# Decay arguments from broadcast running sums in a Mamba-style mixer, instead of small matmuls

## The chip, the core and the metric

The kernel runs on one core of one Trainium2 chip. The metric is the device time of one execution in microseconds (us), median over runs. The core has a matrix engine (TensorE, PE in the profile, with its weight loads as PEld), a vector engine (VectorE, DVE), an activation engine (ScalarE, ACT), a general engine (GpSimd, POOL), a queue engine that here only issues transfers (SyncE, SP), and 16 DMA engines. The engines run side by side and wait for each other through semaphores; each executes its own list in order.

## The reference, cut to what matters

The whole computation is four residual blocks on x of shape (2, 512, 512): a block-sparse linear layer, a quantised feed-forward layer, a state-space mixer, and the feed-forward layer again. The change is in the mixer, which takes most of the time. Per batch, with H=128 heads of P=64 channels, G=8 groups of N=128 states and chunks of CS=128 tokens (four chunks):

```python
proj = hidden @ in_proj_w.T                  # gate z, x, B, C, dt
hBC = silu(conv4(hBC) + conv_b)              # depthwise over 4 tokens
dt = softplus(dt + dt_bias); A_dt = -exp(A_log) * dt
A_cumsum = cumsum(A_dt, axis=-1)             # inside each chunk, per head
Lmat = exp(segment_sum(A_dt))                # exp(cum[l] - cum[s]), 0 above the diagonal
Gm = einsum('clhn,cshn->clsh', C, B)
Y_diag = einsum('clsh,cshp->clhp', Gm * Lmat, x * dt)
states = einsum('clhn,clhp->chpn', B * exp(A_cumsum[-1] - A_cumsum), x * dt)  # carried over chunks
Y_off = einsum('clhn,chpn->clhp', C, states) * exp(A_cumsum)
y = Y_diag + Y_off + D * x;  y = rmsnorm(y) * norm_w * silu(gate);  out = y @ out_proj_w.T
```

The decay argument is the difference cum[l] - cum[s] for every pair of tokens in a chunk, 128 by 128 numbers per head and chunk. The kernel clamps it to at most zero before the exponential; what lies beyond the diagonal is then multiplied by zero in a mask.

## The kernel before, in words

The mixer runs as one block in which every engine has a hand-written list. It works in 128 steps k, one for each pair of heads in each of two batches (K = 128; 64 pairs for each batch). A step of TensorE is, in this order: project x for step k+1 (12 matmuls of 512 columns, L845), `outputs(k-1)` (L907, L913), `arguments(k)` (L870), `turn_x(k)` (L882), on one step in eight the Gram matrices of a new group, project z for k+1 (L845), `states(k)` (L893), on two neighbouring steps in eight a projection of B or C for the next group, and a share of the output projection (L926, 12 matmuls).

ScalarE's list in step k is `w_high` for the next x (L1022), `wo_high` (L1078), `tap` (L1034: first tap of the convolution out of the x projection), `w_high` for the next z, `exponent(k)` (L1060 clamps by Relu, L1062 takes Exp), `y_high` (L1072), `square` (L1066), `activate_x` (L1039), `activate_z` (L1044), and on two steps in eight a third `w_high`, then a `tap` of B or C. VectorE's list is `y_low` (L1249), `accumulate` (L1259), `decay_c` (L1222), `conv` (L1168, three instructions), `scale_x` (L1190, L1195), `gate` (L1239, L1243), `carry` (L1204, L1210), `mask_em` (L1230), and the convolution of B or C. GpSimd's list is `w_low` (L1347), `wo_low` (L1352), `w_low` for z, `sum_squares` (L1362), and on two steps in eight a third `w_low`.

Weights come in 256 KB tiles through two buffers (`w_raw`, NR = 2): SyncE issues the load of a tile only when GpSimd's `w_low` has finished with the tile two before it. PSUM banks for projections are used in a ring of three.

The decay arguments are made on TensorE. Before the steps begin, the running sums `cum` (heads on partitions) are split into three bf16 parts and stored to DRAM (`a_parts`). In each step SyncE loads six rows into `a_right` and six into `a_left` beside rows of ones, and eight bf16 matmuls of 128 columns write both heads' differences into the PSUM tile `ARG`. ScalarE clamps and exponentiates `ARG` in place, 1024 columns at a time. `ce`, a broadcast load of 384 KB of exp(cum), is already made per step by the same queue.

Of the kernel before, what the change touches and what calls it, by code (L numbers as in the profile page):

```python
# [8 lines left out]
BF16 = mybir.dt.bfloat16  # L9
# [38 lines left out]
def build(nc, x_in, mask_t, wa_t, bias_a, w_in, conv_w, conv_b, dt_bias, a_log, d_res, norm_w, w_out,  # L48
          gu_w, gu_z, gu_s, dn_w, dn_z, dn_s, x_mid, e_t, a_parts, out):
    with ExitStack() as ctx:  # L50
# [339 lines left out]
        mask_sb = sb("mask_sb", [P, KT, D], I32)  # L390
# [3 lines left out]
        block_on = sb("block_on", [P, KT * (D // BLK)])  # L394
        scope_a.close()
        early, sb = scope()
        wdt_raw = sb("wdt_raw", [P, KT * P])
# [11 lines left out]
        def load_early(sp):  # L409
            sp.dma_start(cw[:], conv_w).then_inc(m_w, 16)  # L410
            sp.dma_start(cb[:], conv_b).then_inc(m_w, 16)
            sp.dma_start(nw[:], norm_w).then_inc(m_w, 16)
            sp.dma_start(d_col[:], d_res).then_inc(m_w, 16)
            sp.dma_start(dtb_col[:], dt_bias.rearrange("o h -> h o")).then_inc(m_w, 16)
            sp.dma_start(wdt_raw[:], w_in[DT_T]).then_inc(m_w, 16)
            sp.dma_start(w_raw[:, 0], w_in[B_T]).then_inc(w_loaded[0], 16)
            sp.dma_start(w_raw[:, 1], w_in[C_T]).then_inc(w_loaded[1], 16)
# [197 lines left out]
        e_last = sb("e_last", [P, T, H])  # L615
# [14 lines left out]
        a_left = sb("a_left", [P, 2, 2, S], BF16)  # L630
        a_right = sb("a_right", [P, 2, 2, S], BF16)
# [10 lines left out]
        m_xn = sbp("m_xn", [P, 4, D])  # L642
        wdt = sbp("wdt", [P, 2, KT * P], F32R)
# [8 lines left out]
        rest = sbp("rest", [P, B * S])  # L652
        parts = sbp("parts", [P, 3, B * S], BF16)
# [14 lines left out]
        a_in, wdt_hi, wdt_lo = sem("a_log_loaded"), sem("wdt_hi"), sem("wdt_lo")  # L668
# [6 lines left out]
        parts_done, rest_done = sem("parts_done"), sem("rest_done")  # L675
# [5 lines left out]
        a_zero, a_ones = sem("a_zero"), sem("a_ones")  # L681
# [4 lines left out]
        arg_mm, arg_clamped, exp_done, em_done = sem("arg_mm"), sem("arg_clamped"), sem("exp_done"), sem("em_done")  # L686
# [85 lines left out]
        with nc.Block() as block:  # L772
            @block.sync
            def _(sp):
# [8 lines left out]
                def load_args(k):  # L783
                    b, h = batch(k), 2 * pair(k)
                    sp.wait_ge(a_ones, 4)
                    need(sp, arg_mm, k - 1)
                    sp.dma_start(a_right[0:3, k % 2], a_parts[0:3, h:h + 2, b * S:(b + 1) * S])\
                        .then_inc(a_loaded[k % 2], 16)
                    sp.dma_start(a_left[32:35, k % 2], a_parts[0:3, h:h + 2, b * S:(b + 1) * S])\
# [9 lines left out]

                sp.dma_start(a_neg[:], a_log.to_broadcast([P, H])).then_inc(a_in, 16)  # L800
                load_units(-1)
                load_units(0)
                for i in range(3):
                    if i == 2:
                        sp.wait_ge(cum_exp, 3)
                        sp.dma_start(e_t, e_cum[:]).then_inc(scratch_stored, 16)
                    sp.wait_ge(parts_done, i + 1)
                    sp.dma_start(a_parts[i], parts[:, i]).then_inc(scratch_stored, 16)
                sp.wait_ge(scratch_stored, 16 * 4)
# [13 lines left out]
            def _(pe):  # L823
# [40 lines left out]

                def arguments(k):
                    pe.wait_ge(a_loaded[k % 2], 32 * (k // 2 + 1))
                    need(pe, em_done, k)
# [5 lines left out]
                    mm.then_inc(arg_mm, 1)  # L873
# [88 lines left out]

                def spread_last():
# [29 lines left out]
                project(("x", 1))  # L993
                gram(0)
                spread_last()
                turn_dec()
                for k in range(STEPS):
                    if 0 < k < K - 1:
                        project(("x", k + 1))
                    if 1 <= k <= K:  # L1000
                        outputs(k - 1)
                    if k < K:
                        arguments(k)
# [12 lines left out]
            @block.scalar  # L1016
            def _(act):
# [82 lines left out]
                nc.scalar.activation(low[:], low[:], ACT.Ln, bias=1.0).then_inc(softplus, 1)  # L1100
                tap(("b", 0))
# [8 lines left out]
                nc.scalar.activation(parts[:, 0], cum[:].rearrange("p c l -> p (c l)"), ACT.Copy).then_inc(parts_done, 1)  # L1110
                nc.scalar.activation(e_end[:], cum[:, :, CS - 1], ACT.Exp).then_inc(cum_exp, 1)
                act.wait_ge(diff_done, 1)
# [3 lines left out]
                nc.scalar.activation(e_cum[:], cum[:].rearrange("p c l -> p (c l)"), ACT.Exp).then_inc(cum_exp, 1)  # L1116
                act.wait_ge(rest_done, 2)
                nc.scalar.activation(parts[:, 2], rest[:], ACT.Copy).then_inc(parts_done, 1)
# [6 lines left out]
                for b in range(B):  # L1125
                    act.wait_ge(last_mm, b + 1)
                    nc.scalar.activation(e_last[:, b * CPB:(b + 1) * CPB].rearrange("p c h -> p (c h)"), (ST, YT)[b][:],
# [29 lines left out]
            def _(dve):  # L1157
# [41 lines left out]
                def carry(k):  # L1199
# [5 lines left out]
                    for c in range(1, OFFC):  # L1205
                        dve.wait_ge(st_part, (2 * OFFC - 2) * k + 2 * c - 1)
                        for h in range(2):
# [5 lines left out]
                                scalar=e_last[:, batch(k) * CPB + c, at:at + 1],  # L1213
# [97 lines left out]
                dve.wait_ge(parts_done, 1)  # L1311
                nc.vector.tensor_tensor(rest[:], cum[:].rearrange("p c l -> p (c l)"), parts[:, 0], ALU.subtract)                    .then_inc(rest_done, 1)
                dve.wait_ge(parts_done, 2)
                dve.wait_ge(rest_done, 1)
                nc.vector.tensor_tensor(rest[:], rest[:], parts[:, 1], ALU.subtract).then_inc(rest_done, 1)
# [27 lines left out]
            def _(pool):  # L1343
# [10 lines left out]

                def sum_squares(k):
# [8 lines left out]
                nc.gpsimd.memset(a_left[:].bitcast(F32), 0.0).then_inc(a_zero, 1)  # L1364
                nc.gpsimd.memset(a_right[:].bitcast(F32), 0.0).then_inc(a_zero, 1)
                pool.wait_ge(a_zero, 2)
                for j in range(2):
                    nc.gpsimd.memset(a_left[0:3, j], 1.0).then_inc(a_ones, 1)
                    pool.wait_ge(a_ones, 2 * j + 1)
                    nc.gpsimd.memset(a_right[32:35, j], -1.0).then_inc(a_ones, 1)  # L1370
                    pool.wait_ge(a_ones, 2 * j + 2)
                pool.wait_ge(wdt_hi, 1)
                nc.gpsimd.tensor_tensor(wdt[:, 1], wdt_raw[:], wdt[:, 0].bitcast(F32), ALU.subtract).then_inc(wdt_lo, 1)
                w_low(("b", 0))
# [9 lines left out]
                pool.wait_ge(cum_exp, 2)  # L1384
# [3 lines left out]
                for k in range(STEPS):  # L1388
# [140 lines left out]
```

## Time and profile before

| | |
|---|---|
| Median of 3 runs | 2247.12 us (2246.6 to 2247.6) |
| The profiled execution | 2251.26 us, span 2249.5 us |
| PE / PEld / DVE busy | 95% / 78% / 73% |
| ACT / POOL busy | 62% / 40% |
| DMA: moved, share of 16 engines (hardware queue) | 239.72 MB, 33.2% |

The span runs from the first to the last instruction of the profiled execution; the time of that execution has 1.8 us more around it. The mixer's steps run from about 357 us to 1960 us of the span. In the rows, times at the left are starts in us from the span's start, and the second number is how long the merged instructions took; brackets show how long the engine had been idle before and what released it.

### The profile page before, as it was taken

The page shows a single profiled execution, that of the slowest core. Times are in us where ns is not written, and L with a number is a line of the kernel's source. Part 1 is how long each engine was busy: PE and PEld are TensorE (multiplying, and loading weights), DVE is VectorE, ACT ScalarE, POOL GpSimd, SP SyncE. Part 2 cuts the span into 40 slices and gives each one's busy share as a digit, 9 for nine tenths or more (in the row PEclk, how much of TensorE's full clock was granted, in tenths as well). Part 3 has the DMA queues.
Part 4 walks back from the last instruction along what each step waited for, and adds up shares of the span by engine and source line. Part 5 has one row for each costly group of instructions (what it writes and reads, how often), then busy time and mean ns, then how long its engine had stood idle before and what let it go on. Part 6 is the DMA issues. An engine that isn't in the chain of part 4 may idle for free. (4 is left out here: it accounts for less than half of the span.)

```text
span 2249.5 us, 37149 instructions
## 1 busy us (share of the span) xinstructions
PE 2137.5 (95%) x13374; PEld 1765.6 (78%) x13374; DVE 1639.2 (73%) x2683; ACT 1390.0 (62%) x1872; POOL 907.6 (40%) x639
## 2 busy tenths in 40 slices
PE   5999986899999999999999999999999999959999
PEld 4788865788888888888888888888888888748887
DVE  8655466778787777778787777778787877755554
ACT  2222236777777777777777777777777777622221
POOL 2222123454444545454444445454454445342221
PEclk9999988999999999999999999999999999979999
DMA  4434313333333233233333333333332333323431
GB/s 164 138 132 150 103 59 104 101 106 92 111 93 110 97 103 102 94 104 102 101 106 97 107 96 107 96 103 100 95 107 96 107 95 108 120 89 136 168 131 75
DMA packets 127794, 241.87 MB, mean 108 GB/s; under 512 B 13200, under 2 KB 47760, under 8 KB 127376
## 3 DMA queue, kind: packets, MB, share of 16 engines
q1 hardware_dynamic: 127632, 239.72, 33.2%
q8 instruction: 100, 1.64, 0.3%
q14 instruction: 62, 0.51, 0.1%
HBM read 234.17 MB, written 5.51 MB: 107 GB/s over the span
## 5 line engine op out<-in xcount | busy, mean ns | idle before, releaser
L845 PE MATMUL ring<-m_lnt,w_sb 128*128 128x512 f32 x3456 | 853.3, 396 | 15.9 <-DVE xc L1168 15.9
L845 PEld LDWEIGHTS ring<-m_lnt,w_sb 128*128 128x128 f32 x3456 | 639.1, 189 | 149.3 <-DVE xc L1168 19.6
L1347 POOL TENSOR_TENSOR w_sb<-w_raw,w_sb 128x512 fp32r<-128x512 f32 x288 | 434.6, 1514 | 337.0 <-ACT w_sb L1022 336.5
L1168 DVE SCALAR_TENSOR_TENSOR xc<-ring,cw,xc 128x511 f32<-128x511 f32 (+2 forms) x384 | 287.3, 748 | 185.7 <-ACT xc L1034 176.7
L926 PE MATMUL ring<-wo,ygs 128*128 128x512 f32 x1536 | 383.1, 399 | 2.5 <-POOL wo L1352 2.5
L1362 POOL TENSOR_TENSOR ysq<-ysq,y 128x512 f32<-128x512 f32 x126 | 163.8, 1300 | 531.3 <-ACT y L1066 531.3
L926 PEld LDWEIGHTS ring<-wo,ygs 128*128 128x128 f32 x1536 | 282.5, 189 | 60.7 <-issue 3.1
L1022 ACT ACTIVATE w_sb<-w_raw 128x512 fp32r<-128x512 f32 x288 | 177.1, 621 | 33.6 <-DMA w_raw<-w_in 33.6
L1034 ACT ACTIVATE xc<-ring,cb,cw 128x512 f32<-128x512 f32 x128 | 99.2, 775 | 146.8 <-PE ring L845 146.8
L1060 ACT ACTIVATE arg<-arg 128x1024 f32<-128x1024 f32 x128 | 129.0, 1008 | 90.4 <-PE arg L870 90.4
L907 PE MATMUL yt<-em,x_dt 128*64 128x128 f32 x2048 | 183.6, 279 | 1.2 <-DVE em L1230 1.2
L365 PE MATMUL bank_e<-f_lnt,f_gu 128*128 128x512 f32 x672 | 159.8, 399 | 11.2 <-DVE f_lnt L135 6.5
L1352 POOL TENSOR_TENSOR wo<-wo_raw,wo 128x512 fp32r<-128x512 f32 x128 | 168.6, 1317 | 3.3 <-ACT wo L1078 3.3
L288 POOL TENSOR_TENSOR f_gu<-f_gu_f,f_gu 128x1024 fp32r<-128x1024 f32 x28 | 67.3, 2404 | 251.8 <-ACT f_gu L312 251.8
L1062 ACT ACT_TABLE_LOAD x128 | 164.2, 1283 | 2.4
L1039 ACT ACT_TABLE_LOAD x127 | 162.9, 1283 | 2.3
L365 PEld LDWEIGHTS bank_e<-f_lnt,f_gu 128*128 128x128 f32 x672 | 130.1, 194 | 39.7 <-issue 10.5
L365 PE MATMUL bank<-f_lnt,f_gu 128*128 128x512 f32 x672 | 154.1, 390 | 3.4 <-DVE f_hf L251 1.8
L1230 DVE TENSOR_TENSOR em<-arg,gt 128x1024 f32<-128x1024 f32 x128 | 155.9, 1218 | 0.1
L907 PEld LDWEIGHTS yt<-em,x_dt 128*64 128x64 f32 x2048 | 118.0, 136 | 46.4 <-issue 43.3
L365 PEld LDWEIGHTS bank<-f_lnt,f_gu 128*128 128x128 f32 x672 | 125.9, 188 | 30.3 <-issue 4.0
L913 PE MATMUL yt<-ce,state 128*64 128x128 f32 x1536 | 149.1, 273 | 0.0
(178 smaller groups left out, 3131.3 us busy)
## 6 DMA issues: line engine op xcount, KB each, us to landing
w_raw<-w_in SPq DMA_DIRECT2D x288, 256.0 KB, 4.4
ce<-e_t SPq DMA_DIRECT2D x128, 384.0 KB, 4.3
wo_raw<-w_out SPq DMA_DIRECT2D x128, 256.0 KB, 4.5
f_gu_q<-gu_w SPq DMA_DIRECT2D x28, 512.0 KB, 5.3
f_gu_zr<-gu_z SPq DMA_DIRECT2D x28, 512.0 KB, 6.6
f_gu_sr<-gu_s SPq DMA_DIRECT2D x28, 512.0 KB, 8.0
f_dn_q<-dn_w SPq DMA_DIRECT2D x28, 256.0 KB, 7.1
f_dn_zr<-dn_z SPq DMA_DIRECT2D x28, 256.0 KB, 7.5
```

The source lines that it names most:

```text
L365: mm = nc.tensor.matmul(dst[half][:], gu[:, j, b, c:c + P], lnt[:, a, k, half * TOK:(half + 1) * TOK], start=(i == 0), stop=(i == 3 * KT - 1))
L845: mm = nc.tensor.matmul(dst[:], w_sb[:, u % WR, wp, k * P:(k + 1) * P], lnt[:, xp, k, b * S:(b + 1) * S], start=(i == 0), stop=(i == 3 * K ...
L907: mm = nc.tensor.matmul(YT[h * HD:(h + 1) * HD, c * CS:(c + 1) * CS], x_dt[:, at:at + HD], em[:, h, c * CS:(c + 1) * CS], start=True, stop ...
L926: mm = nc.tensor.matmul(dst[:], ygs[:, j % OR, yp, t * P:(t + 1) * P], wo[:, j % WOR, wp], start=(m == 0), stop=(m == 3 * HALF - 1))
L1022: nc.scalar.activation(w_sb[:, u % WR, 0], w_raw[:, u % NR], ACT.Copy).then_inc(w_hi, 1)
L1039: nc.scalar.activation(xc[:, k % 3], xc[:, k % 3], ACT.Silu).then_inc(silu_x, 1)
L1062: nc.scalar.activation(part, part, ACT.Exp, scale=-1.0).then_inc(exp_done, 1)
L1168: nc.vector.scalar_tensor_tensor(out=dst[:, d:S], in0=src[:, 0:S - d], scalar=cw[:, tile, j:j + 1], in1=dst[:, d:S], op0=ALU.mult, op1=ALU ...
L1230: nc.vector.tensor_tensor(em[:], ARG[:], gt[:, k // QG % 2].rearrange("p (o t) -> p o t", o=1).to_broadcast([P, 2, S]), ALU.mult).then_inc ...
L1347: nc.gpsimd.tensor_tensor(w_sb[:, u % WR, 1], w_raw[:, u % NR], w_sb[:, u % WR, 0].bitcast(F32), ALU.subtract).then_inc(w_lo, 1)
L1352: nc.gpsimd.tensor_tensor(wo[:, j % WOR, 1], wo_raw[:, j % 2], wo[:, j % WOR, 0].bitcast(F32), ALU.subtract).then_inc(wo_lo, 1)
L1362: nc.gpsimd.tensor_tensor(part, part, y[:, k % 2], ALU.add).then_inc(ysq_done, 1)
```

## The change

The matmuls of the decay argument, their operands, the bf16 split and the memsets that prepared the operands are taken out. In their place:

- The running sums are stored to DRAM once as they are (`a_t`), and each step loads both heads' rows, 512 tokens each, broadcast over all 128 partitions into `a_row` (512 KB). The load waits for `exp_done` of two steps back.
- Before the steps, TensorE transposes `cum` once (8 transposes) and VectorE copies the result into `a_q`, a column for each step, chunk and head.
- `exponent(k)`: ScalarE takes Relu of a_q - a_row for the first head, four instructions of 128 columns with a per-partition bias, then Exp of it (512 columns, into PSUM), waits for GpSimd, and takes Exp of the second head.
- `clamp_second(k)`: GpSimd subtracts a_q from a_row and takes the minimum with 0 for the second head, four instructions of 128 columns. It stands behind `w_low` of the z tile.
- `e_cum` is exponentiated earlier in the preparation; `wdt_raw` is loaded at the start of the mixer instead of long before it, so the first weights are split in another order; `e_last` keeps two of four chunks for each batch.

```diff
 load_args(k):
-    sp.wait_ge(a_ones, 4)
-    need(sp, arg_mm, k - 1)
-    sp.dma_start(a_right[0:3, k % 2], a_parts[0:3, h:h + 2, b * S:(b + 1) * S])...
-    sp.dma_start(a_left[32:35, k % 2], a_parts[0:3, h:h + 2, b * S:(b + 1) * S])...
+    need(sp, exp_done, k - 1)
+    sp.dma_start(a_row[:, k % 2], a_t[h:h + 2, b * S:(b + 1) * S]
+                 .rearrange("(o h) t -> o h t", o=1).to_broadcast([P, 2, S]))...
...
 TensorE, before the steps:
+    for b in range(B):
+        for c in range(CPB):
+            mm = nc.tensor.transpose(ARG[:, b, c * H:(c + 1) * H], cum[:, b * CPB + c], ident[:])
 TensorE, each step:
-    for h in range(2):
-        for c in range(CPB):
-            mm = nc.tensor.matmul(ARG[:, h, c * CS:(c + 1) * CS],
-                                  a_left[:, k % 2, h, c * CS:(c + 1) * CS],
-                                  a_right[:, k % 2, h, c * CS:(c + 1) * CS], start=True, stop=True)
...
 exponent(k):
-    act.wait_ge(arg_mm, k + 1)
-    part = ARG[:].rearrange("p h t -> p (h t)")
-    nc.scalar.activation(part, part, ACT.Relu, scale=-1.0).then_inc(arg_clamped, 1)
-    act.wait_ge(arg_clamped, k + 1)
-    nc.scalar.activation(part, part, ACT.Exp, scale=-1.0).then_inc(exp_done, 1)
+    act.wait_ge(a_loaded[k % 2], 16 * (k // 2 + 1))
+    need(act, em_done, k)
+    for c in range(CPB):
+        nc.scalar.activation(a_row[:, k % 2, 0, c * CS:(c + 1) * CS],
+                             a_row[:, k % 2, 0, c * CS:(c + 1) * CS], ACT.Relu,
+                             bias=a_q[:, k, c, 0:1], scale=-1.0).then_inc(arg_first, 1)
+    act.wait_ge(arg_first, CPB * (k + 1))
+    nc.scalar.activation(ARG[:, 0], a_row[:, k % 2, 0], ACT.Exp, scale=-1.0)
+    act.wait_ge(arg_second, CPB * (k + 1))
+    nc.scalar.activation(ARG[:, 1], a_row[:, k % 2, 1], ACT.Exp).then_inc(exp_done, 1)
...
+clamp_second(k), on GpSimd behind w_low of the z tile and ahead of sum_squares(k - 1):
+    pool.wait_ge(a_loaded[k % 2], 16 * (k // 2 + 1))
+    for c in range(CPB):
+        nc.gpsimd.tensor_scalar(a_row[:, k % 2, 1, c * CS:(c + 1) * CS],
+                                a_row[:, k % 2, 1, c * CS:(c + 1) * CS],
+                                a_q[:, k, c, 1:2], 0.0, ALU.subtract, ALU.min).then_inc(arg_second, 1)
...
 ScalarE, before the steps (a copy of each of the three parts, Exp of e_cum in between):
-    nc.scalar.activation(parts[:, 0], cum..., ACT.Copy).then_inc(parts_done, 1)
     nc.scalar.activation(e_end[:], cum[:, :, CS - 1], ACT.Exp).then_inc(cum_exp, 1)
+    nc.scalar.activation(e_cum[:], cum..., ACT.Exp).then_inc(cum_exp, 1)
     act.wait_ge(diff_done, 1)
     nc.scalar.activation(diff[:], diff[:], ACT.Exp).then_inc(cum_exp, 1)
-    act.wait_ge(rest_done, 1)
-    nc.scalar.activation(parts[:, 1], rest[:], ACT.Copy).then_inc(parts_done, 1)
-    nc.scalar.activation(e_cum[:], cum..., ACT.Exp).then_inc(cum_exp, 1)
-    act.wait_ge(rest_done, 2)
-    nc.scalar.activation(parts[:, 2], rest[:], ACT.Copy).then_inc(parts_done, 1)
```

## Rows read from the trace of the kernel before

**Rows 1.** Windows, one stretch of the steps: busy time and count of each engine, clock, DMA.

```profile
600.00:900.00 300.00, 296.97 (x2061) 246.90 (x2060) 237.11 (x401) 228.75 (x304) 143.50 (x102) 1.00 0.33 100
```

**Rows 2.** Waits, 600 to 1500 us: total us, times, longest.

```profile
ACT arg L1060 <- PE arg L870: 50.5, 54, 0.9
...
ACT w_sb L1022 <- DMA w_raw<-w_in: 16.8, 8, 2.2
```

**Rows 3.** Timeline of an ordinary step (PEld left out).

```profile
860.22 0.78 ACT L1034 ACTIVATE xc<-ring,cb,cw 128x512 f32<-128x512 f32 x1 [1.31 <-PE ring L845]
...
861.59 1.27 POOL L1347 TENSOR_TENSOR w_sb<-w_raw,w_sb 128x512 fp32r<-128x512 f32 x1
861.79 0.62 PE L870 MATMUL arg<-a_right,a_left 128*128 128x128 bf16 x8
...
862.25 0.61 PE L882 MATMUL xt<-ident,xc 128*128 128x128 f32 x4
...
862.45 1.01 ACT L1060 ACTIVATE arg<-arg 128x1024 f32<-128x1024 f32 x1 [0.94 <-PE arg L870]
...
863.26 0.55 DVE L1190 TENSOR_TENSOR x_dec<-xt,dec_q 128x384 f32<-128x384 f32 x1
...
864.77 1.01 ACT L1062 ACTIVATE arg<-arg 128x1024 f32<-128x1024 f32 x1
865.10 0.75 DVE L1243 SCALAR_TENSOR_TENSOR sz<-y,nw,sz 128x512 f32<-128x512 f32 x1
865.46 0.83 PE L893 MATMUL st<-x_dec,b_tok 128*128 128x128 f32 x6
865.88 0.63 ACT L1072 ACTIVATE ygs<-sz 128x512 fp32r<-128x512 f32 x1
...
869.88 0.95 DVE L1222 TENSOR_TENSOR ce<-ce,bc 128x768 f32<-128x768 f32 x1
...
873.39 0.62 PE L870 MATMUL arg<-a_right,a_left 128*128 128x128 bf16 x8
```

**Rows 4.** Timeline of the two steps with B and C projections (PEld left out).

```profile
897.95 0.63 ACT L1022 ACTIVATE w_sb<-w_raw 128x512 fp32r<-128x512 f32 x1 [2.16 <-DMA w_raw<-w_in]
...
898.66 1.30 POOL L1347 TENSOR_TENSOR w_sb<-w_raw,w_sb 128x512 fp32r<-128x512 f32 x1 [1.02 <-ACT w_sb L1022]
...
900.81 1.01 ACT L1062 ACTIVATE arg<-arg 128x1024 f32<-128x1024 f32 x1
...
906.53 2.32 DVE L1168 SCALAR_TENSOR_TENSOR bc<-ring,cw,bc 128x511 f32<-128x511 f32 x3 [2.96 <-ACT bc L1034]
...
910.76 2.03 DVE L1222 TENSOR_TENSOR ce<-ce,bc 128x768 f32<-128x768 f32 x1
...
915.54 0.94 PE L893 MATMUL st<-x_dec,b_tok 128*128 128x128 f32 x6 [0.81 <-DVE x_dec L1190]
```

**Rows 5.** Groups of instructions by shape, GpSimd: count, busy us, mean ns.

```profile
L115 POOL TENSOR_SCALAR f_n_xn<-xr,f_n_mv,f_n_rstd 128x512 f32<-128x512 f32 x8 | 16.9, 2124 | 30.5 <-DVE f_n_rstd L109 24.8 <-PE bank_e L123 5.7
...
L1360 POOL COPY ysq<-y 128x512 f32<-128x512 f32 x2 | 1.2, 612 | 8.5 <-ACT y L1066 8.5
```

**Rows 6.** Groups of instructions by shape, ScalarE.

```profile
L1034 ACT ACTIVATE xc<-ring,cb,cw 128x512 f32<-128x512 f32 x128 | 99.2, 775 | 146.8 <-PE ring L845 146.8
...
L1044 ACT ACT_TABLE_LOAD x1 | 1.3, 1283 | 0.0
...
L1095 ACT ACTIVATE a_neg<-a_neg 128x128 f32<-128x128 f32 x1 | 0.3, 313 | 0.0
```

**Rows 7.** Timeline of the preparation before the first step.

```profile
334.79 0.60 ACT L1108 ACTIVATE cum<-arg 128x512 f32<-128x512 f32 x1 [0.30 <-PE arg L959]
...
348.44 1.05 ACT L1049 ACTIVATE bc<-bc 128x1024 f32<-128x1024 f32 x1
...
349.54 2.08 PE L855 MATMUL ring<-bc 128*128 128x128 f32 x8 [12.05 <-ACT bc L1049]
```

**Rows 8.** The page's DMA queue: packets, MB, share of 16 engines.

```profile
q1 hardware_dynamic: 127632, 239.72, 33.2%
```

More of the change, by code:

```diff
@@ L8 @@
 F32R = mybir.dt.float32r
-BF16 = mybir.dt.bfloat16
 I32 = mybir.dt.int32
@@ L394, in build @@
         block_on = sb("block_on", [P, KT * (D // BLK)])
+        mask_sb = sb("mask_sb", [P, KT, D], I32)
         scope_a.close()
         early, sb = scope()
-        wdt_raw = sb("wdt_raw", [P, KT * P])
         cw = sb("cw", [P, CONV // P, TAPS])
@@ L614, in build @@
         dec_q = sb("dec_q", [P, K, CPB, 2])
-        e_last = sb("e_last", [P, T, H])
+        a_q = sb("a_q", [P, K, CPB, 2])
+        e_last = sb("e_last", [P, B * (OFFC - 1), H])
         banks_ctx.close()
@@ L629, in build @@
         b_tok = sb("b_tok", [P, 2, OFFC * NS])
-        a_left = sb("a_left", [P, 2, 2, S], BF16)
-        a_right = sb("a_right", [P, 2, 2, S], BF16)
+        a_row = sb("a_row", [P, 2, 2, S])
         ce = sb("ce", [P, 2, 2, OFFC * CS])
@@ L642, in build @@
         m_xn = sbp("m_xn", [P, 4, D])
+        wdt_raw = sbp("wdt_raw", [P, KT * P])
         wdt = sbp("wdt", [P, 2, KT * P], F32R)
@@ L651, in build @@
         e_cum = sbp("e_cum", [P, B * S])
-        rest = sbp("rest", [P, B * S])
-        parts = sbp("parts", [P, 3, B * S], BF16)
         e_end = sbp("e_end", [P, T])
@@ L685, in build @@
         gram_mm, btok_mm, gt_done, btok_done = sem("gram_mm"), sem("btok_mm"), sem("gt_done"), sem("btok_done")
-        arg_mm, arg_clamped, exp_done, em_done = sem("arg_mm"), sem("arg_clamped"), sem("exp_done"), sem("em_done")
+        arg_first, arg_second = sem("arg_first"), sem("arg_second")
+        exp_done, em_done = sem("exp_done"), sem("em_done")
         xt_mm, xdt_done, xdec_done = sem("xt_mm"), sem("xdt_done"), sem("xdec_done")
@@ L802, in _ @@
                 load_units(0)
[L803 to L809, printed above, removed]
+                sp.wait_ge(cum_done, B)
+                sp.dma_start(a_t, cum[:].rearrange("p c l -> p (c l)")).then_inc(scratch_stored, 16)
+                sp.wait_ge(cum_exp, 2)
+                sp.dma_start(e_t, e_cum[:]).then_inc(scratch_stored, 16)
+                sp.wait_ge(scratch_stored, 16 * 2)
                 load_args(0)
@@ L961, in cumulate, with turn_cum @@
                         mm.then_inc(cum_mm, 1)
+                def turn_cum():
+                    pe.wait_ge(cum_done, B)
+                    for b in range(B):
+                        for c in range(CPB):
+                            mm = nc.tensor.transpose(ARG[:, b, c * H:(c + 1) * H], cum[:, b * CPB + c], ident[:])
+                        mm.then_inc(cumt_mm, 1)
                 def spread_last():
@@ L993, in _ @@
                 project(("x", 1))
+                turn_cum()
                 gram(0)
@@ L1002, in _ @@
                     if k < K:
-                        arguments(k)
                         turn_x(k)
@@ L1089, in _ @@
                 w_high(("b", 0))
+                act.wait_ge(wdt_loaded, 16)
+                nc.scalar.activation(wdt[:, 0], wdt_raw[:], ACT.Copy).then_inc(wdt_hi, 1)
                 for t in range(T):
@@ L1100, in _ @@
                 nc.scalar.activation(low[:], low[:], ACT.Ln, bias=1.0).then_inc(softplus, 1)
+                act.wait_ge(m_w, 16 * 5)
                 tap(("b", 0))
@@ L1109, in _ @@
                 act.wait_ge(cum_done, B)
-                nc.scalar.activation(parts[:, 0], cum[:].rearrange("p c l -> p (c l)"), ACT.Copy).then_inc(parts_done, 1)
                 nc.scalar.activation(e_end[:], cum[:, :, CS - 1], ACT.Exp).then_inc(cum_exp, 1)
+                nc.scalar.activation(e_cum[:], cum[:].rearrange("p c l -> p (c l)"), ACT.Exp).then_inc(cum_exp, 1)
                 act.wait_ge(diff_done, 1)
                 nc.scalar.activation(diff[:], diff[:], ACT.Exp).then_inc(cum_exp, 1)
-                act.wait_ge(rest_done, 1)
-                nc.scalar.activation(parts[:, 1], rest[:], ACT.Copy).then_inc(parts_done, 1)
-                nc.scalar.activation(e_cum[:], cum[:].rearrange("p c l -> p (c l)"), ACT.Exp).then_inc(cum_exp, 1)
-                act.wait_ge(rest_done, 2)
-                nc.scalar.activation(parts[:, 2], rest[:], ACT.Copy).then_inc(parts_done, 1)
                 tap(("x", 1))
@@ L1126, in _ @@
                     act.wait_ge(last_mm, b + 1)
-                    nc.scalar.activation(e_last[:, b * CPB:(b + 1) * CPB].rearrange("p c h -> p (c h)"), (ST, YT)[b][:],
+                    nc.scalar.activation(e_last[:, b * (OFFC - 1):(b + 1) * (OFFC - 1)].rearrange("p c h -> p (c h)"),
+                                         (ST, YT)[b][:, H:OFFC * H],
                                          ACT.Copy).then_inc(last_done, 1)
@@ L1212, in carry @@
                                 in0=state[:, c - 1, h * HD:(h + 1) * HD],
-                                scalar=e_last[:, batch(k) * CPB + c, at:at + 1],
+                                scalar=e_last[:, batch(k) * (OFFC - 1) + c - 1, at:at + 1],
                                 in1=ST[:, c * PAIR + h * HD:c * PAIR + (h + 1) * HD],
@@ L1310, in _ @@
                 conv(("x", 0))
[L1311 to L1315, printed above, removed]
+                for b in range(B):
+                    dve.wait_ge(cumt_mm, b + 1)
+                    nc.vector.tensor_copy(a_q[:, b * JP:(b + 1) * JP],
+                                          ARG[:, b].rearrange("p (c j h) -> p j c h", c=CPB, h=2)).then_inc(aq_done, 1)
                 mask_gram(0)
@@ L1353, in wo_low, with clamp_second @@
                                             ALU.subtract).then_inc(wo_lo, 1)
+                def clamp_second(k):
+                    pool.wait_ge(a_loaded[k % 2], 16 * (k // 2 + 1))
+                    if k == 0:
+                        pool.wait_ge(aq_done, B)
+                    for c in range(CPB):
+                        nc.gpsimd.tensor_scalar(a_row[:, k % 2, 1, c * CS:(c + 1) * CS],
+                                                a_row[:, k % 2, 1, c * CS:(c + 1) * CS],
+                                                a_q[:, k, c, 1:2], 0.0, ALU.subtract, ALU.min).then_inc(arg_second, 1)
                 def sum_squares(k):
@@ L1362, in sum_squares @@
                         nc.gpsimd.tensor_tensor(part, part, y[:, k % 2], ALU.add).then_inc(ysq_done, 1)
[L1364 to L1371, printed above, removed]
+                w_low(("b", 0))
                 pool.wait_ge(wdt_hi, 1)
                 nc.gpsimd.tensor_tensor(wdt[:, 1], wdt_raw[:], wdt[:, 0].bitcast(F32), ALU.subtract).then_inc(wdt_lo, 1)
-                w_low(("b", 0))
                 w_low(("c", 0))
@@ L1395, in _ @@
                         w_low(unit)
+                    if k < K:
+                        clamp_second(k)
                     if 1 <= k <= K:
```

28 lines of the change are left out of this document (10 added, 18 removed).

## The prediction, as it was put on record

> **What bounds the kernel now.** I read the table of stretches first. In 300 us of the steps TensorE is busy 296.97 us at a granted clock of 1.00, while VectorE has 237, ScalarE 229 and GpSimd 143.5 [rows 1]. So the mixer is bound by TensorE's list, and a shorter list is worth something as long as the other lists keep up. The waits then show how near they are. In 900 us ScalarE waits 50.5 us for the argument matmuls and 16.8 us, in 8 waits of up to 2.2 us, for a weight tile [rows 2]. Those 8 waits recur once in eight steps, so I looked at two timelines: an ordinary step, and the two neighbouring steps that also project B or C.
>
> In the ordinary step two starts of L870 lie 873.39 - 861.79 = 11.60 us apart, and TensorE stands still nowhere for another engine. Its nearest dependence is `x_dec`: VectorE has it at 863.81, TensorE asks at 865.46, a slack of 1.65 us. ScalarE has two holes, 1.31 us before `tap` and 0.94 us before L1060 [rows 3]. In the other two steps it is different. ScalarE takes the z tile only at 897.95, after 2.16 us of waiting for its DMA; everything in its list behind that is late, the convolution of B starts after 2.96 us of idleness, and at 915.54 TensorE waits 0.81 us for `x_dec` [rows 4]. I call these the chain steps; with the Gram step behind them they are three of eight. The last group has none, so there are 15 such groups, and about 80 ordinary steps of the 128 are left after the irregular first ones.
>
> **What goes from TensorE.** From the first argument matmul to the first transpose is 862.25 - 861.79 = 0.46 us [rows 3]; the 0.62 us of the group's busy time overlaps the next one. The wait on semaphores ahead of the arguments now stands ahead of `turn_x`, and I charge about 0.05 us for it, an estimate. That leaves 0.41 us a step. In 80 ordinary steps this is 33 us; in all steps but the first it would be 52 us.
>
> **What ScalarE gets.** Out go two instructions of 1.01 us; in come four Relus of 128 columns and two Exps of 512. The nearest rows for a Relu are 0.313 us (128 columns, no scalar from memory) and 0.775 us (512 columns, two scalars from memory) [rows 6]; I take 0.38 us each, and 0.28 from start to start since successive rows of this engine overlap by about 0.1. That makes about 1.15 us, and 0.5 to 0.6 for an Exp. With the table load of 1.28 between them [rows 6] this is about 0.3 us more than before. The 0.94 us hole ahead of it is gone, because `a_row` has long been loaded, so alone it costs nothing in an ordinary step; cover gone, it would be 0.3 us in each of 45 chain steps at most, 14 us.
>
> **What GpSimd gets, and what waits for it.** This is the disputed price. The trace has no clamp of 128 columns. The one tensor-with-scalar instruction on GpSimd takes 2.1 us for 512 columns; the copy takes 0.61 [rows 5]. Scaled by columns with 0.1 us fixed, one clamp is 0.6 us by the first and 0.23 by the second. If nothing of the first shrinks with the columns it is 2.1. I take c = 0.6 us, since it is the same operation with another second step, and keep 0.15 to 2.1 as bounds.
>
> Four clamps start when `w_low` of z ends, and the second Exp, 0.62 us, waits for all four, with 0.05 us for the hand-over (both estimates). Ordinary step: 861.59 + 1.27 + 0.05 + 4c + 0.62 = 863.53 + 4c, so 865.93 for c = 0.6. `y_high` started at 865.88 anyway, because it waits for `sz`, which VectorE ends at 865.85 [rows 3]. So nothing moves. ScalarE's own round becomes 11.60 - 1.31 - (865.88 - 863.53) + 4c = 7.94 + 4c, or 10.3 us for c = 0.6, against a TensorE round of 11.60 - 0.41 = 11.19. It fits until c = 0.81.
>
> Chain step: the z tile comes late from DMA, and that time is set by GpSimd and the queue, not by TensorE. `w_low` ends at 899.96, so the second Exp ends at 900.63 + 4c = 903.03, where it ended at 901.82 before [rows 4]. That is 4c - 1.19 = 1.2 us later, and behind the Exp stand `y_high`, `square`, both Silus, the next two weight tiles and the tap of B; then the convolutions and `x_dec`. TensorE already waits at this place, so the delay arrives, and TensorE's own saving in the three steps is spent in waiting. 15 x 1.2 = 18 us lost.
>
> The Trainium skill speaks for a smaller c: its page "GPSIMD Engine Reference", section "Engine selection", says that one-input elementwise work on GpSimd runs roughly at line rate, and section "Elementwise" gives 769 ns for 512 elements as its best case. An estimate from that figure is 0.2 to 0.25 us per clamp, and the sum would end at -34 us in place of -21. The row of 2.1 us for 512 columns speaks against it.
>
> **Port and queues.** `decay_c`, with both inputs in SBUF, takes 0.95 us in the ordinary step [rows 3] and 2.03 us in a chain step that is otherwise the same [rows 4], where a `w_low` of GpSimd runs at the time; the three instructions of `conv`, with one input in PSUM, take 2.32 us in total. The clamps lie from 862.9 to 865.3, over `conv`, `scale_x` and the first `gate` instruction, which read PSUM; only `sz` at 865.10 may be held, for about 0.2 us, within the slack. I charge nothing. On SyncE `a_row` stands where the two small loads stood and waits for an older event than `ce` behind it does. It adds 128 x 0.524 = 67 MB to 239.72 MB that take 33.2% of the DMA engines [rows 8]: in proportion that is 9.3 points more, about 43%. No queue fills; the price is only a burst. The critical z tile is issued before the next `a_row`, so I charge nothing; if a tile did wait behind one, it would be 0.524 MB at 321 GB/s (239.72 MB in 0.332 x 2249.5 us) = 1.6 us, 24 us over 15 groups.
>
> **The preparation.** From 334.79 to 348.44 ScalarE makes the sums, three bf16 parts with two waits for VectorE, and the activations for the first Gram matrix, and TensorE stands 12.05 us [rows 7]. Without the parts ScalarE's list is cum, a table load 1.28, `e_end` at about 0.2 and `e_cum` and `diff` at 1.01 each like L1060, a tap of 0.78, a weight tile of 0.63, a table load 1.28, a Silu of z at 0.6 [rows 3, 4, 6]: from 335.39 on that is 6.8 us, and the Silu of B and C starts at about 342 instead of 348.44. That is 6 us; the first clamp group gives perhaps 1 back, the removed memsets and the moved weight load change the start by under 1 in either direction. The 8 transposes and two copies of `a_q` fall into the hole. I take -6.
>
> **Sum.** -33 + 18 - 6 = -21 us against the profiled execution's 2251.3 us, which is 4.1 us above the median; against the median of 2247.1 us that is 2226 us. With c from 0.52 to 0.67 and 6 us for the rest of the terms the likeliest case spans 2214 to 2240.
>
> **Rivals.**
> 1. *Short clamps.* At c = 0.25 the chain steps lose only ScalarE's own 0.3 us: -33 + 5 - 6 = -34, so 2213 us. For it: the copy row, and the page named above. Against it: the row of 2.1 us. Chance 0.17.
> 2. *The whole saving arrives.* If the chain steps are in truth set by TensorE, 52 us and the 6 come in full: 2189 us. For it: its wait there is only 0.81 us [rows 4]. Against it: the DMA wait ahead of them does not depend on TensorE. Chance 0.10.
> 3. *Slower: GpSimd becomes the bound.* If a large part of the 2.1 us is fixed, c exceeds 0.81, ScalarE's round 7.94 + 4c passes TensorE's, and the sum crosses zero near c = 0.83. At c = 1.0: 80 x 0.34 + 15 x 2.81 - 6 = +63, so 2310 us; at 2.1 it is over 2700. For it: it is four instructions where the row has one, each with its own start and its own scalar. Against it: the copy shows no large fixed part. Chance 0.17.
> 4. *The burst.* Loads of 512 KB hold weight tiles back: -21 + 24 = +3, so 2250 us, no change. For it: 16.8 us of waits for these tiles already [rows 2]. Against it: the order of issue. Chance 0.08.
>
> My forecast has 0.45, and 0.03 is left for the rest. A difference under 0.2%, 4.5 us, cannot be told from none. Faster: 0.45 + 0.17 + 0.10 = 0.72; within 0.2%: 0.08; slower: 0.20. The range goes from 2190, the edge of rival 2, to 2265, which takes in rival 4 and rival 3 up to c of about 0.87.
>
> **What would show it.** L870 is gone and ordinary steps are 11.2 us apart (if 11.6 or more: rival 3). A clamp takes 0.6 us; the second Exp ends at most 0.1 us before `y_high`. In the chain steps the wait of TensorE for `x_dec` or a bank grows to some 2 to 3 us per group, and ScalarE's wait for GpSimd appears before the second Exp. The wait of 12.05 us before the first Gram matrix halves. ScalarE's waits for `w_raw` stay near 17 us per 900 (if they double: rival 4). The prediction fails most easily by c, at 60 us of time for each us of c, and far more beyond 0.81.

## The result: 2303 us, slower

| | before | after |
|---|---|---|
| Median of 4 runs | 2246.99 us | 2302.97 us (2297.41 to 2311.72) |
| Ratio, 95% interval | | 1.0242, 1.0224 to 1.026 |
| The profiled execution | 2251.26 us, span 2249.5 | 2311.72 us, span 2310.0 |

The profiled execution is the longest of the four. The predicted time was 2226 us, the range ended at 2265. The page of the changed kernel, busy time of the engines and the DMA queue (beside the table ahead of the prediction and [rows 8]):

```profile
PE 2112.5 (91%) x12358; PEld 1717.4 (74%) x12358; DVE 1738.3 (75%) x2683; ACT 1419.5 (61%) x2381; POOL 1257.3 (54%) x1145
...
q1 hardware_dynamic: 159856, 305.00, 40.5%
```

One stretch of its windows, which answers to [rows 1]:

```profile
600.00:900.00 300.00, 276.91 (x1787) 225.24 (x1786) 246.26 (x384) 225.95 (x382) 198.36 (x188) 1.00 0.42 135
```

TensorE has 25 us less work in all and is no longer busy throughout: 277 of 300 us, at the same granted clock. GpSimd has 350 us more. Its waits from 600 to 1500 us, beside [rows 2]:

```profile
ACT arg L1059 <- POOL a_row L1353: 151.4, 69, 2.6
...
PE st L876 <- DVE x_dec L1184: 28.2, 29, 2.2
...
ACT w_sb L1012 <- DMA w_raw<-w_in: 24.6, 14, 2.7
...
PE ring L838 <- ACT sz L1034: 23.9, 9, 2.8
```

The wait for the argument matmuls, 50.5 us, is gone, and one of 151.4 us for GpSimd stands in its place: every Exp of the second head waits (69 times in 900 us, which are 68 to 69 steps of 13.1 us on average). Behind it TensorE waits for `x_dec` and for a bank that a late Silu of z holds. The new instructions, by shape:

```profile
L1353 POOL TENSOR_SCALAR a_row<-a_row,a_q 128x128 f32<-128x128 f32 x512 | 404.6, 806 | 0.0
...
L1053 ACT ACTIVATE a_row<-a_row,a_q 128x128 f32<-128x128 f32 x512 | 162.5, 392 | 0.0
```

A clamp takes 0.81 us, not 0.6; a Relu 0.39, as reckoned. The timeline of an ordinary step shows what the clamps close (TensorE, VectorE and weight loads left out):

```profile
871.12 0.60 ACT L1059 ACTIVATE arg<-a_row 128x512 f32<-128x512 f32 x1 [2.56 <-POOL a_row L1353]
...
875.12 0.62 ACT L1012 ACTIVATE w_sb<-w_raw 128x512 fp32r<-128x512 f32 x1
...
875.82 1.50 POOL L1340 TENSOR_TENSOR w_sb<-w_raw,w_sb 128x512 fp32r<-128x512 f32 x1 [1.66 <-ACT w_sb L1012]
...
877.28 1.30 POOL L1345 TENSOR_TENSOR wo<-wo_raw,wo 128x512 fp32r<-128x512 f32 x1
...
878.54 1.29 POOL L1340 TENSOR_TENSOR w_sb<-w_raw,w_sb 128x512 fp32r<-128x512 f32 x1
...
879.81 3.25 POOL L1353 TENSOR_SCALAR a_row<-a_row,a_q 128x128 f32<-128x128 f32 x4
...
883.09 0.60 ACT L1059 ACTIVATE arg<-a_row 128x512 f32<-128x512 f32 x1 [2.56 <-POOL a_row L1353]
```

From one step's Exp of the second head to the next step's is a closed round (a chain of work that leads from an instruction back to the same one a step later) with no gap in it: ScalarE from the Exp to the high part of the next x tile, 4.70 us up to GpSimd's start; three subtractions, 3.99; four clamps, 3.25; hand-over 0.03. That is 11.97 us, where TensorE alone would need 11.17. The step with the late tile, beside [rows 4]:

```profile
915.21 0.63 ACT L1012 ACTIVATE w_sb<-w_raw 128x512 fp32r<-128x512 f32 x1 [2.46 <-DMA w_raw<-w_in]
...
917.18 3.22 POOL L1353 TENSOR_SCALAR a_row<-a_row,a_q 128x128 f32<-128x128 f32 x4
...
920.43 0.60 ACT L1059 ACTIVATE arg<-a_row 128x512 f32<-128x512 f32 x1 [1.51 <-POOL a_row L1353]
...
924.59 2.79 PE L838 MATMUL ring<-m_lnt,w_sb 128*128 128x512 f32 x11 [2.56 <-ACT sz L1034]
```

TensorE stands 2.56 us there for the Silu of z, which follows the late Exp in ScalarE's list. The preparation, beside [rows 7]:

```profile
345.11 2.08 PE L848 MATMUL ring<-bc 128*128 128x128 f32 x8 [4.53 <-ACT bc L1039]
```

The hole of 12.05 us is now 4.53. In this execution the first transpose of step 0 starts 4.6 us earlier than before, from there to the first transpose of the last step it takes 63.2 us more, and what follows takes 1.9 us more: 60.5 us, the difference of the two spans. Where the 63.2 lie is seen from the starts of the first transpose of each step, which I took from the traces. The table has the mean distance to the next step by place in the group of eight, over 14 groups (the first and the last left out); places 3 to 5 are the chain steps.

| us | 0 | 1 | 2 | 3 | 4 | 5 | 6 | 7 | group |
|---|---|---|---|---|---|---|---|---|---|
| before | 11.60 | 11.60 | 11.60 | 14.32 | 14.77 | 13.82 | 11.60 | 11.60 | 100.91 |
| after | 11.15 | 11.91 | 11.92 | 18.64 | 15.39 | 13.78 | 11.17 | 11.17 | 105.13 |
| e1 | 11.17 | 11.17 | 11.17 | 13.94 | 16.46 | 13.45 | 11.17 | 11.17 | 99.68 |
| e2 | 11.17 | 11.17 | 11.17 | 14.31 | 16.54 | 13.24 | 11.17 | 11.17 | 99.93 |
| e3 | 13.56 | 13.40 | 13.29 | 16.02 | 16.50 | 18.22 | 11.17 | 12.32 | 114.49 |
| e4 | 11.16 | 11.89 | 11.91 | 18.50 | 15.49 | 13.81 | 11.17 | 11.17 | 105.10 |
| e5 | 11.17 | 11.17 | 11.17 | 13.89 | 15.51 | 13.88 | 11.17 | 11.17 | 99.11 |
| e6 | 11.17 | 11.17 | 11.17 | 14.25 | 16.86 | 13.24 | 11.17 | 11.17 | 100.18 |
| e7 | 11.17 | 11.17 | 11.17 | 13.89 | 16.09 | 13.67 | 11.17 | 11.17 | 99.48 |
| e8 | 11.17 | 11.17 | 11.17 | 14.39 | 16.18 | 13.55 | 11.17 | 11.17 | 99.96 |
| e9 | 11.17 | 11.91 | 11.87 | 16.51 | 16.95 | 13.13 | 11.17 | 11.17 | 103.87 |
| e10 | 11.18 | 11.86 | 11.17 | 15.28 | 17.31 | 12.83 | 11.17 | 11.17 | 101.97 |
| e11 | 11.17 | 11.17 | 11.17 | 13.89 | 14.07 | 13.88 | 11.17 | 11.17 | 97.67 |
| e12 | 11.60 | 11.60 | 11.60 | 14.32 | 14.32 | 12.82 | 11.60 | 11.60 | 99.46 |

Three ordinary places (6, 7 and 0) got TensorE's 0.43 us. Places 1 and 2 lost 0.3 each to the round, and place 3 lost 4.3. The round is as long in those three places as in the others: from one Exp of the second head to the next it is 11.9 to 12.0 us in places 5, 6, 7, 0 and 1 (means over the same groups). Behind the chain steps TensorE comes late and the round has slack; at 11.17 us a step for TensorE it loses 0.8 us of that slack in each of places 6, 7 and 0, and from place 1 on TensorE waits for it.

The clock is not the cause. In its steps (all but the first 20 us of them) the changed kernel spent 24 us at the lower level, a granted clock of 0.50, that is 1.2 GHz, and the kernel before 3 us; but e1 below has the same 24 us and is some 80 us faster.

### The profile page after: what moved, and what is told of

Read it like the earlier page. It is cut to its first block and busy times, and to the rows that moved or that the text cites. A ratio compares the mean times of both kernels' runs of the same rounds, so it can differ in the third digit from the quotient of the medians.

```text
span 2310.0 us, 35876 instructions
## 1 busy us (share of the span) xinstructions
PE 2112.5 (91%) x12358; PEld 1717.4 (74%) x12358; DVE 1738.3 (75%) x2683; ACT 1419.5 (61%) x2381; POOL 1257.3 (54%) x1145
## 5 line engine op out<-in xcount | busy, mean ns | idle before, releaser
L1340 POOL TENSOR_TENSOR w_sb<-w_raw,w_sb 128x512 fp32r<-128x512 f32 x288 | 393.9, 1372 | 362.8 <-ACT w_sb L1012 362.8
L1353 POOL TENSOR_SCALAR a_row<-a_row,a_q 128x128 f32<-128x128 f32 x512 | 404.6, 806 | 0.0
L1059 ACT ACTIVATE arg<-a_row 128x512 f32<-128x512 f32 x128 | 77.1, 602 | 278.8 <-POOL a_row L1353 278.8
L1243 DVE TENSOR_TENSOR ygs<-sz,ygs 128x512 fp32r<-128x512 f32 x128 | 199.3, 1557 | 0.7 <-ACT ygs L1069 0.7
L876 PEld LDWEIGHTS st<-x_dec,b_tok 128*128 128x128 f32 x768 | 100.7, 193 | 89.2 <-DVE x_dec L1184 84.9
L876 PE MATMUL st<-x_dec,b_tok 128*128 128x128 f32 x768 | 113.9, 285 | 57.6 <-DVE x_dec L1184 57.5
L1053 ACT ACTIVATE a_row<-a_row,a_q 128x128 f32<-128x128 f32 x512 | 162.5, 392 | 0.0
```

The source lines that it names most:

```text
L876: mm = nc.tensor.matmul(ST[:, c * PAIR:(c + 1) * PAIR], b_tok[:, k // QG % 2, c * NS:(c + 1) * NS], x_dec[:, c * PAIR:(c + 1) * PAIR], sta ...
L1243: nc.vector.tensor_tensor(ygs[:, k % OR, 1], sz[:, k % 3], ygs[:, k % OR, 0].bitcast(F32), ALU.subtract).then_inc(yg_lo, 1)
L1340: nc.gpsimd.tensor_tensor(w_sb[:, u % WR, 1], w_raw[:, u % NR], w_sb[:, u % WR, 0].bitcast(F32), ALU.subtract).then_inc(w_lo, 1)
L1353: nc.gpsimd.tensor_scalar(a_row[:, k % 2, 1, c * CS:(c + 1) * CS], a_row[:, k % 2, 1, c * CS:(c + 1) * CS], a_q[:, k, c, 1:2], 0.0, ALU.su ...
```

## The experiments

Medians of four runs each, beside the median of the kernel before on the same chip at the time (2245.4 for e1 to e4, 2247.1 for e5 to e8, 2244.8 for e9 to e12). The changed kernel's 2303.0 was measured beside 2247.0, so up to some 2 us of a difference between groups of runs can be the chip's.

### e1 to e4: clamps, their wait, their engine, the loads

e1, no clamps of the second head:

```diff
-                    act.wait_ge(arg_second, CPB * (k + 1))
...
-                    if k < K:
-                        clamp_second(k)
```

> The changed kernel without the four GpSimd clamps and without the wait for them: the second head's exponential is taken of the loaded sums as they are, so its decay argument is left out of the computation. Theory G (the clamps close a round through GpSimd: weight high part on ScalarE, three subtractions and four clamps on GpSimd, Exp, the next weight high part, 8.7 us and four clamps of 0.81, and they also make the step after the late weight tile longer): ordinary steps 11.17 us apart in all places, the step with the late tile near 14.4, the whole 2205 to 2220 us. Theory D (the 512 KB load of each step holds weight tiles back): the time stays above 2280 us, with ScalarE's waits for weight tiles near 25 us per 900.

Measured 2221.5 us, ratio 0.9896 (0.988 to 0.9913). All ordinary places are at 11.17, place 3 is at 13.94 (14.4 was expected): theory G holds, D falls. The total is 1.5 us above what I gave; place 4 is longer than I thought.

e2, the same clamps one step ahead:

```diff
+                clamp_second(0)
                 for k in range(STEPS):
...
-                    if k < K:
-                        clamp_second(k)
+                    if k + 1 < K:
+                        clamp_second(k + 1)
```

> All of the computation, the same four clamps on GpSimd at the same place of its list, but for the second head of the next step, so that no exponential waits for the clamps just issued. Theory G: the wait is the cost and not GpSimd's time as such, so nearly all comes back: 2205 to 2225 us, ScalarE's wait for GpSimd ahead of the second Exp gone. Rival P (GpSimd's added 3.2 us of work delays weights or holds VectorE's instructions with two inputs in SBUF): 2250 us or more. Theory D: above 2280 us.

Measured 2230.0 us, 0.9932 (0.9916 to 0.9949), 5 us above what theory G gave: some 70 us of the changed kernel's time gone with GpSimd's work unchanged. It was the wait, not the work. Rival P has a small part: 8.5 us above e1.

e3, the clamps on VectorE:

```diff
                         decay_c(k)
+                        clamp_second(k)        # nc.vector, waits and operands as on GpSimd
                     if k + 1 < K:
                         conv(("x", k + 1))
```

> All of the computation, the four clamps of the second head on VectorE between decay_c and the convolution of x, where VectorE had a hole of 1.79 us in an ordinary step. Theory G: a clamp of 128 columns is short there (0.2 to 0.3 us, a guess from the 0.54 us of VectorE's 512-column instruction of this kind), so 2205 to 2225 us. If VectorE's list is as near to TensorE's as GpSimd's was: x_dec late, 2235 us or more. Theory D: above 2280 us.

Measured 2450.4 us, 1.0911 (1.0892 to 1.0929), a miss of over 200 us by theory G. The other branch, `x_dec` late, came true (TensorE waits 72.1 us for it from 600 to 1500 us), but with no upper bound it foretold little. The tile's durations (minimum, median, maximum in ns) and a stretch of the timeline show why:

```profile
L1225 DVE TENSOR_SCALAR a_row<-a_row,a_q x512: 271/1298/1371, 347.0 to 2146.7; 128x128 f32<-128x128 f32 x171
```

```profile
910.91 1.50 POOL L1350 TENSOR_TENSOR w_sb<-w_raw,w_sb 128x512 fp32r<-128x512 f32 x1 [1.65 <-ACT w_sb L1012]
911.20 3.99 DVE L1225 TENSOR_SCALAR a_row<-a_row,a_q 128x128 f32<-128x128 f32 x4
...
912.37 1.28 POOL L1355 TENSOR_TENSOR wo<-wo_raw,wo 128x512 fp32r<-128x512 f32 x1
...
913.61 1.30 POOL L1350 TENSOR_TENSOR w_sb<-w_raw,w_sb 128x512 fp32r<-128x512 f32 x1
```

The 211 clamps that overlap no GpSimd instruction take 0.274 us on average; the 301 that do have a median of 1.31 us (mean 1.26), the length of one GpSimd subtraction. While GpSimd subtracts three tiles in a row, four clamps need 3.99 us: three of them let one whole instruction pass each, and the fourth takes 0.27. The lower clock has a small part in e3: its steps have 140 us at the lower level, those of e7 14. Over e3's 14 groups each us at that level goes with 0.12 us more, so an estimate of its share is 15 us.

e4, the rows loaded for two steps only:

```diff
-                    need(sp, exp_done, k - 1)
-                    sp.dma_start(a_row[:, k % 2], ...)
+                    if k < 2:
+                        sp.dma_start(a_row[:, k % 2], ...)
```

> The changed kernel with the rows of sums loaded only for the first two steps; all later steps work on what lies in the buffers, so their decay arguments are left out of the computation; every clamp and wait between the engines stays. Theory G: 2295 to 2305 us, as changed. Theory D: the 67 MB are the cost, so 2240 us or less, and ScalarE's waits for weight tiles fall to 17 us per 900 or less.

Measured 2302.8 us, 1.0254 (1.0237 to 1.0271): the changed kernel's time. Theory D is out; the 67 MB cost nothing that can be measured in this kernel.

### e5 to e8: the ceiling, a dose, two other ways

e5, the kernel before without the matmuls:

```diff
                     if k < K:
-                        arguments(k)
                         turn_x(k)
...
-                    act.wait_ge(arg_mm, k + 1)
+                    act.wait_ge(a_loaded[k % 2], 32 * (k // 2 + 1))
+                    need(act, em_done, k)
```

> The kernel before with the eight argument matmuls of each step left out (the decay argument is then not computed; ScalarE clamps and exponentiates what lies in ARG, with waits for the loads and for mask_em instead); GpSimd, the DMAs and ScalarE's two instructions of 1024 columns stay. It prices TensorE's part alone. Theory G with the chain steps set elsewhere: ordinary steps 11.17 us apart and the three others as long in sum as before, so 34 us saved, 2205 to 2215 us. Rival F (the whole saving arrives, 0.43 us in 127 steps): 2190 to 2196 us.

Measured 2220.5 us, 0.9883 (0.9867 to 0.99): 26.7 us saved, so the time is 5.5 us above my band. Ordinary steps give 0.43 us each, and the three chain steps are 0.37 us longer in sum than before (43.28 against 42.91). So what the matmuls are worth there is all waited away, as the prediction had it, and rival F, its rival 2, is out.

e6, one clamp of 512 columns:

```diff
-                    for c in range(CPB):
-                        nc.gpsimd.tensor_scalar(a_row[:, k % 2, 1, c * CS:(c + 1) * CS], ..., a_q[:, k, c, 1:2], ...)
+                    nc.gpsimd.tensor_scalar(a_row[:, k % 2, 1], a_row[:, k % 2, 1], a_q[:, k, 0, 1:2], ...)
```

> The changed kernel with one clamp of 512 columns for each step in place of four of 128 (all four chunks take the column of the first, so the decay arguments of three chunks are not the right ones). A dose: GpSimd spends 2.1 us in place of 3.2. Theory G: the round through GpSimd falls from 11.92 to about 10.8 us, under TensorE's 11.17, so ordinary steps come at 11.17 throughout (1.5 us a group), and the step with the late tile loses 1.1 us: 15 x 2.6 = 39 us less, about 2264 us. Rival P (the port shared with VectorE decides): one long instruction holds VectorE longer than four short ones, 2290 us or more.

Measured 2230.8 us, 0.9921 (0.9905 to 0.9938):

```profile
L1352 POOL TENSOR_SCALAR a_row<-a_row,a_q x128: 1978/1997/2707, 351.1 to 1931.8; 128x512 f32<-128x512 f32 x128
```

The ordinary steps did what theory G said. But I gave 1.1 us to place 3 and it fell by 4.4; the total is 33 us under my 2264, and the response to 1.2 us of GpSimd's time is 72 us. Once the round is under TensorE's, no lag is left to carry into place 3. From 128 and 512 columns the price of a clamp follows: 0.705 us (the trace's shortest are 0.702) and 1.997, so 3.4 ns a column and 0.27 us fixed; the 0.81 on average in the changed kernel includes 118 clamps of 0.79 to 1.4 us, 108 of which overlap the second `gate` instruction of VectorE; the 30 that overlap none take 0.71.

e7, VectorE again, at another place:

```diff
                         mask_em(k)
+                    if k + 1 < K:
+                        clamp_second(k + 1)    # nc.vector
```

> All of the computation, the clamps of the second head on VectorE as in e3, but for the next step and behind mask_em, where GpSimd has nothing to do. Theory P for e3 (a VectorE clamp takes 0.27 us, and 1.3 us only where it must let a whole GpSimd subtraction pass): nearly all clamps take 0.27 us, ordinary steps 11.17 us, 2215 to 2230 us. Rival V (VectorE's own list is too long by the clamps): x_dec late, ordinary steps over 11.5 us, 2260 us or more.

Measured 2219.8 us, 0.9874 (0.9857 to 0.989), the time of e5. The same instructions as in e3, 230 us apart by their place in VectorE's list (some 15 of them the clock's):

```profile
L1225 DVE TENSOR_SCALAR a_row<-a_row,a_q x512: 269/278/1367, 347.7 to 1917.7; 128x128 f32<-128x128 f32 x171
```

e8, one subtraction for both heads:

```diff
+                    nc.gpsimd.tensor_tensor(part, part, a_q[:, k].rearrange("p c (h o) -> p h c o", o=1)
+                                            .to_broadcast([P, 2, CPB, CS]), ALU.subtract).then_inc(arg_second, 1)
...
+                    nc.scalar.activation(row, row, ACT.Relu, scale=-1.0).then_inc(arg_first, 1)
+                    act.wait_ge(arg_first, k + 1)
+                    nc.scalar.activation(part, row, ACT.Exp, scale=-1.0).then_inc(exp_done, 1)
```

> All of the computation in another form: one GpSimd subtraction of 1024 columns for both heads with a_q broadcast over columns, one step ahead, then one Relu and one Exp of 1024 columns on ScalarE. GpSimd about 2.4 us a step in place of 3.0, ScalarE about 0.3 us less than in the changed kernel. If ScalarE's longer list is what the chain steps lose in e1 and e2: 2208 to 2220 us. If the port decides (a two-input subtraction holds VectorE longer): 2230 us or more.

Measured 2230.0 us, 0.9922 (0.9906 to 0.9939), the time of e2 and at the edge of its rival's band. The subtraction is shorter than thought (median 1.905 us), ScalarE's list is too, and nothing came of it. So ScalarE's extra 0.3 us is not what the chain steps lose in e2; what e2 and e8 share and e7 lacks is GpSimd's work and, in 900 us, 39.6 us (e8) and 44.7 us (e2) in which GpSimd waits for the row load. The runs don't part the two.

### e9 to e12: what makes place 3 so long, and what sets the chain steps

e9 and e10 leave the clamps out at place 3, or at places 1 and 2:

```diff
+        def clamped(k):
+            return k % QG not in (3,)          # e10: (1, 2)
...
-                    if k < K:
+                    if k < K and clamped(k):
                         clamp_second(k)
```

> The changed kernel without the clamps, and the wait for them, in one step of eight: the one with the late weight tile (its second head's argument is then not made). Theory G1 (that step's growth by 4.3 us is mostly its own clamps standing behind the late tile): the step falls from 18.6 to about 14.5 to 15.5 us and the next by a little, 2245 to 2255 us. Theory G2 (the growth is lag carried in from the two steps ahead): the step stays above 17 us, 2280 us or more.

> The changed kernel without the clamps in the two steps ahead of the late tile (their second head's argument is then not made). Both fall from 11.92 to 11.17 us, 1.5 us a group. Theory G1: the step with the late tile stays at 17.5 us or more, 2275 to 2282 us. Theory G2: it falls to 15.5 or less, 2250 us or less.

Measured: e9 2286.8 us, 1.0196 (1.0177 to 1.0215); e10 2259.2 us, 1.007 (1.0053 to 1.0087). Of the two places that were to fall to 11.17 in e10 only place 2 did; place 1 stays at 11.86, because its lag comes from the clamps of the steps ahead of it, which are still there. Places 3 to 5 sum to 47.81 us in the changed kernel, 46.59 in e9, 45.42 in e10 and 43.85 in e1. Of the 3.96 us that clamps cost there, those of place 3 bring 1.2, and those of the two steps ahead bring 2.4 as lag carried in. Neither theory was right in full: G2 gave the larger part, but place 3 fell to 16.5 in e9, and e10's total is 9 us above G2's bound.

e11 is e7, and e12 the kernel before, with the third weight tile's high part ahead of the Silus:

```diff
                         square(k - 1)
+                    for unit in ahead[2:]:
+                        w_high(unit)
                     if k + 1 < K:
                         activate_x(k + 1)
                         activate_z(k + 1)
-                    for unit in ahead[2:]:
-                        w_high(unit)
```

> e7 (all of the computation, clamps on VectorE a step ahead) with one more edit: on the two steps of eight that bring a third weight tile, ScalarE makes its high part ahead of the two Silus and not behind them, some 2 us earlier, so the next z tile is loaded earlier. If the late tile sets the three chain steps: ScalarE's waits for weight tiles fall from 20 us per 900 to under 8, the group from 99.5 us to 97 to 98.5, 2190 to 2208 us. If VectorE's chain sets them by itself: 2218 us or more.

> The kernel before with the same edit alone (the third high part ahead of the Silus). TensorE waits about 1.4 us a group there, so at most 20 us can come: 2230 to 2240 us if the late tile sets those waits, 2247 us if not.

Measured: e11 2196.2 us, 0.9781 (0.9765 to 0.9798); e12 2231.2 us, 0.9943 (0.9927 to 0.996). Both as the late-tile theory had it. From 600 to 1500 us ScalarE waits for weight tiles as follows in e11, against 20.3 us in e7:

```profile
ACT w_sb L1012 <- DMA w_raw<-w_in: 0.7, 3, 0.2
```

TensorE's matmuls no longer wait for `x_dec` (17.2 us in e7), and place 4 falls from 16.09 to 14.07. e11 beats both kernels, by 49 us and by some 105. On top of e12 the argument's new form is worth 35 us.

## Why the prediction was wrong

**What bounds, and what TensorE gives: right.** 0.41 us a step was forecast, 0.43 is measured; that ordinary steps get it and chain steps don't is shown by e5.

**ScalarE's Relus and Exps: right** (0.39 and 0.60 us). **The queues: right**, by e4; ScalarE's waits for weight tiles rose from 16.8 to 24.6 us per 900, as much without the row loads (23.8). **The preparation: right**; the hole shrank by 7.5 us, and from the last copy of the running sums to the first transpose of step 0 it is 16.5 us where it was 23.3, so 6.8 for the forecast 6. In the profiled execution only 4.6 of them show, because its running sums came 2.2 us later.

**The price of a clamp: mis-sized**, 0.81 for 0.6. I scaled the 512-column row with 0.1 us fixed, from rows of other operations; e6 gives 0.27 fixed. With that a clamp alone is 0.7; the other 0.1 is overlap with VectorE's instructions, which I charged at nothing.

**"ScalarE's own round becomes 7.94 + 4c ... It fits until c = 0.81": the step that failed.** With the measured c this formula still gives 11.18 us and no loss in ordinary steps. I had subtracted ScalarE's hole of 1.31 us ahead of `tap` as free. It isn't on the path: after the high part of x the round leaves ScalarE and runs through GpSimd's three subtractions, which start with that high part whatever ScalarE does meanwhile. The round is 8.7 + 4c, it passes TensorE's at c = 0.62, and at 0.81 it is 11.9. The rows of the kernel before could have told: from `y_high` at 865.88 to the end of the z subtraction at 873.19 + 1.27 it is 8.58 us, and with hand-over and Exp 9.25 + 4c, which is above 11.19 even at my own c of 0.6. It came out shorter, at 8.7, mainly because the first subtraction takes 1.50 us in the changed kernel and took 1.91 before, where more of it overlapped `decay_c`:

```profile
870.07 1.91 POOL L1347 TENSOR_TENSOR w_sb<-w_raw,w_sb 128x512 fp32r<-128x512 f32 x1 [1.65 <-ACT w_sb L1022]
```

The prediction read the 0.95 us of `decay_c` in the ordinary step as the time without a neighbour; a subtraction of GpSimd overlaps it there too, and there it is GpSimd's that gets longer. In both steps the one that starts first keeps its time: `decay_c` at 869.88 ahead of 870.07, and in the chain step the subtraction at 910.71 (1.27 us) ahead of `decay_c` at 910.76.

Rival 3, with GpSimd as the bound, was the right mechanism at the wrong point; it got 0.17 and a first loss at 0.81. That its 2310 us lies near the measured time is luck: it belongs to c = 1.0.

**"4c - 1.19 = 1.2 us later" for a chain group: the second failure.** With the measured c it gives 2.0; measured is 4.90 for places 3 to 5. It took the z tile's time as fixed. The tile's load hangs on the subtraction of the third weight tile of the step ahead (in the changed kernel that ends at 912.64 and the load is issued at 912.67), so lag of that step comes in with it: 2.4 of the 3.96 us by e10. The remainder between these parts, some 0.35 us, and the split of the 0.94 that e1 still loses there stay open.

By groups: forecast -2.05 for ordinary and +1.2 for chain steps, measured -0.68 and +4.90. The fifteen groups make 63 us where -13 was forecast. A slip in the sum, without weight here: c from 0.52 to 0.67 and 6 us either way give 2215 to 2236 us, not 2214 to 2240.

**The rule on GpSimd.** The Trainium skill's page "GPSIMD Engine Reference", section "Engine selection", has one-input work roughly at line rate. The trace disagrees for this instruction: 1.997 us for 512 columns (e6) and 0.705 for 128, where the copy of 512 columns took 0.612 [rows 5]. The row of 2.1 us that I set against it was the better guide.

## What to carry to other kernels

To test whether added work fits, walk the whole round from an instruction to its next occurrence through every engine that it passes; a hole in one engine's list is slack only if the path runs through it. If a round exceeds the bound engine's by a little, the lag adds up from step to step; slack hides it for a while, and then it comes out in the places where something is already late. Here 0.8 us a step became 4.3 us at place 3. Work whose input is there early can be issued a step ahead: that alone was worth some 70 us here.

## What the runs showed of the hardware

A VectorE clamp of 128 columns takes 0.27 us alone and 1.3 beside a GpSimd subtraction: with both engines' lists full they took turns by whole instruction, so that the short instruction paid for the long one (e3 against e7, some 215 us). On GpSimd this tensor-with-scalar instruction costs 0.27 us and 3.4 ns a column, so 3.8 us for 1024 columns, an estimate; a two-input subtraction with its second input broadcast over columns took 1.905 us for 1024 (e8).
